# Eight of seventeen one-hot matrices per body made by ScalarE instead of VectorE, in a two-layer graph network with attention and experts

## The reference, cut to what matters

```python
def _rgcn_layer(X, W, root, bias, gamma, beta, src, dst, etype, inv_deg):   # first stage, four layers
    h = jnp.einsum('ni,rio->rno', X, W)
    msg = h[etype, src] * inv_deg[:, None]
    agg = jax.ops.segment_sum(msg, dst, num_segments=X.shape[0])
    out = agg + X @ root + bias
    ...                                       # layer norm, gamma, beta
    out = jax.nn.elu(out)
    return out + X

all_h = jnp.einsum('ni,rio->nro', h, weight)  # second stage, once, eight relations, no weights
msg = all_h[src, rel]
agg = jax.ops.segment_sum(msg, dst, num_segments=h.shape[0])
```

## Time and profile before

| | |
|---|---|
| Three runs | 8418.92, 8429.41 (median), 8451.86 us |
| The profiled execution | 8445.94 us, of which the span from first to last instruction is 8444.1 us |
| Granted TensorE clock, mean | 0.832 of full |
| Busy, share of the span | TensorE 5985.2 us, 71%; VectorE 4887.0 us, 58%; GpSimd 4238.0 us, 50%; ScalarE 1584.5 us, 19% |
| Four layers | from 622.7 to about 5522 us |
| Last graph stage | about 6530 to 7576 us |
| One-hots L524 and L526 | 3332 and 833, 1127.5 and 225.2 us busy |
| Sums L544 | 4165, 1746.5 us busy |
| Gathers L515 | 4165, 4015.2 us busy |
| Step products L559 | 3142.9 us busy |

### The profile page before, as it was taken

The page is one execution under the profiler, slowest core; times in us unless marked ns, Lnnn a source line. Parts: engine busy times, 40 slices in busy tenths (PEclk is TensorE's granted clock), DMA queues, the critical chain, the costliest instruction groups (busy, mean ns, idle before and its releaser), DMA issues. The chain is left out here.

```text
span 8444.1 us, 107673 instructions
## 1 busy us (share of the span) xinstructions
PE 5985.2 (71%) x18474; PEld 3592.9 (43%) x18474; DVE 4887.0 (58%) x16836; ACT 1584.5 (19%) x3834; POOL 4238.0 (50%) x4288
## 2 busy tenths in 40 slices
PE   0587777767777767777776777778488677664398
PEld 0244444444544444444443333345334444443265
DVE  7106666667777767777776677732433666662412
ACT  0231112211111113333330000022021111110132
POOL 0007677756666656666656777710000777762211
PEclk9799899988788888889887666679699888877699
DMA  1324444433333333434434333300034333330000
GB/s 54 127 93 124 120 125 124 125 118 113 112 112 114 113 117 114 118 116 119 119 111 127 104 104 104 103 24 0 0 129 138 105 105 105 105 92 2 12 14 17
DMA packets 457906, 797.23 MB, mean 94 GB/s; under 512 B 87260, under 2 KB 322100, under 8 KB 457609
## 3 DMA queue, kind: packets, MB, share of 16 engines
q0 software_dynamic: 200480, 548.02, 22.9%
q1 hardware_dynamic: 257382, 248.75, 8.9%
HBM read 606.70 MB, written 189.74 MB: 94 GB/s over the span
## 5 line engine op out<-in xcount | busy, mean ns | idle before, releaser
L515 POOL DMA_INDIRECT gnn_msg<-tables,gnn_row_ring x4165 | 4015.2, 964 | 2346.5 <-issue 1644.2
L559 PE MATMUL bank<-gnn_msg,gnn_hot 128*128 128x256 f32 x8330 | 3142.9, 496 | 1292.5 <-DVE sums L544 1030.5
L559 PEld LDWEIGHTS bank<-gnn_msg,gnn_hot 128*128 128x128 f32 x8330 | 1715.7, 235 | 2586.6 <-DVE sums L544 1928.3
L544 DVE TENSOR_TENSOR sums<-sums,bank 128x256 f32 x4165 | 1746.5, 419 | 1587.6 <-PE bank L559 1127.2
L524 DVE TENSOR_SCALAR gnn_hot<-iota,gnn_meta_ring 128x128 f32<-128x128 f32 x3332 | 1127.5, 356 | 332.0 <-ACT gnn_meta_ring L508 332.0
L133 POOL TENSOR_TENSOR ve<-mv,eps 128x7 f32<-128x7 f32 x35 | 7.2, 205 | 1348.3 <-DVE mv L127 1199.7
L652 PE MATMUL bank<-gnn_w,residual 128*128 128x512 f32 x1176 | 572.5, 611 | 1.4 <-ACT residual L668 1.4
L507 ACT COPY gnn_row_ring<-row 128x9 int32 (+1 forms) x490 | 97.8, 200 | 1512.7 <-PE bank L559 1498.8
L1698 PE MATMUL bank<-tables_w,sums 128*128 128x512 f32 x784 | 338.3, 593 | 6.4 <-ACTq L117 6.4
L652 PEld LDWEIGHTS bank<-gnn_w,residual 128*128 128x128 f32 x1176 | 237.2, 202 | 174.7 <-issue 152.9
L672 ACT COPY residual<-bank 128x512 f32<-128x512 f32 x294 | 172.3, 586 | 681.3 <-PE bank L652 681.3
(11 more groups left out here) (398 smaller groups left out, 6804.7 us busy)
## 6 DMA issues: line engine op xcount, KB each, us to landing
tables<-residual SPq DMA_DIRECT2D x294, 256.0 KB, 2.7
gnn_msg<-tables,gnn_row_ring POOLq DMA_INDIRECT x4165, 2.8
tables<-sums SPq DMA_DIRECT2D x98, 512.0 KB, 2.9
tables<-gnn_msg SPq DMA_DIRECT2D x98, 256.0 KB, 2.1
residual<-first_norm SPq DMA_DIRECT2D x98, 128.0 KB, 3.1
first_norm<-state SPq DMA_DIRECT2D x1, 6272.0 KB, 20.8
first_rows<-residual SPq DMA_DIRECT2D x1, 6272.0 KB, 39.0
mixer_rows<-residual SPq DMA_DIRECT2D x49, 128.0 KB, 2.4
```

What stands on the lines that cost most here:

```text
L515: self.nc.gpsimd.indirect_dma_start(out=self.msg[:, s0 + u, :], out_offset=None, in_=table, in_offset=bass.IndirectOffsetOnAxis(ap=self.ro ...
L544: self.nc.vector.tensor_tensor(at, at, self.sums(s), ALU.add).then_inc(self.added, 1)
L559: self.nc.tensor.matmul(self.sums(s), self.hot[:, s, :], self.msg[:, s, :], start=True, stop=True).then_inc(self.summed, 1)
```

## The change

`ACT_HOTS` (4) of the one-hots of each half are made by ScalarE, in `ring`, behind its two copies. The distance |column - node| goes to a new buffer `away` (Abs with the scale -1 and the node's number as bias); the one-hot is Relu(weight - weight x distance), for which a third column of `meta_ring` holds the negated weights. Without weights it is Relu(1 - distance). VectorE makes the first five one-hots of the first half and the first four of the second, nine in a body where it made seventeen, by a new `NEXT_HOTS`; `begin_vector` makes five. TensorE waits for one of two counters, according to who made the one-hot. The rest of the program is the same.

```diff
-NEXT_HOTS = (((), (0,), (1,), (2,), (3,), (4,), (5,), (6,), (7,)),
-             ((), (), (0, 1), (2,), (3,), (4, 5), (6,), (7, 8)))
+DVE_HOTS = (5, 4)
+ACT_HOTS = 4
+NEXT_HOTS = (((), (), (0,), (), (1,), (), (2,), (), (3,)),
+             ((), (), (0,), (1,), (), (2,), (3,), (4,)))
...
     def ring(self, act, i, n, h):
 
         s0, w = HALVES[h]
+        m = self.meta_ring[:, h, 0:w, :]
         act.wait_ge(self.summed, n * SLOTS + (s0 + w))
         gate(act, self.c)
         at = ds(i * SLOTS + s0, w)
         self.nc.scalar.copy(self.row_ring[:, h, 0:w], self.rows[:, at]).then_inc(self.ring_ready, 1)
-        self.nc.scalar.copy(self.meta_ring[:, h, 0:w, :], self.c.meta[:, at, :]).then_inc(self.ring_ready, 1)
+        self.nc.scalar.copy(m[:, :, 0:2], self.c.meta[:, at, :]).then_inc(self.ring_ready, 1)
+        act.wait_ge(self.ring_ready, n * 4 + (2 * h + 2))
+        gate(act, self.c)
+        for k in range(ACT_HOTS):
+            u = DVE_HOTS[h] + k
+            self.nc.scalar.activation(self.away[:, k, :], self.c.iota[:], ACT.Abs, bias=m[:, u, 0:1], scale=-1.0)\
+                .then_inc(self.away_ready, 1)
+        if self.weighted:
+            self.nc.scalar.mul(m[:, :, 2], m[:, :, 1], -1.0).then_inc(self.away_ready, 1)
+        else:
+            act.sem_inc(self.away_ready, 1)
+        act.wait_ge(self.away_ready, (n * 2 + (h + 1)) * (ACT_HOTS + 1))
+        gate(act, self.c)
+        for k in range(ACT_HOTS):
+            u = DVE_HOTS[h] + k
+            to = self.hot[:, s0 + u, :]
+            if self.weighted:
+                ins = self.nc.scalar.activation(to, self.away[:, k, :], ACT.Relu, bias=m[:, u, 1:2], scale=m[:, u, 2:3])
+            else:
+                ins = self.nc.scalar.activation(to, self.away[:, k, :], ACT.Relu, bias=self.c.ones[:, 0:1], scale=-1.0)
+            ins.then_inc(self.act_hot_ready, 1)
...
     def begin_vector(self, dve, n):
 
         dve.wait_ge(self.ring_ready, n * 4 + 2)
-        for u in range(HALF):
+        for u in range(DVE_HOTS[0]):
             self.one_hot(0, u)
...
     def tensor(self, pe, n, after):
         for s in range(SLOTS):
             pe.wait_ge(self.landed[s], n * 16 + 16)
-            pe.wait_ge(self.hot_ready, n * SLOTS + s + 1)
+            h = 0 if s < HALF else 1
+            u = s - HALVES[h][0]
+            if u < DVE_HOTS[h]:
+                pe.wait_ge(self.hot_ready, n * sum(DVE_HOTS) + (h * DVE_HOTS[0] + u + 1))
+            else:
+                pe.wait_ge(self.act_hot_ready, n * 2 * ACT_HOTS + (h * ACT_HOTS + u - DVE_HOTS[h] + 1))
```

More of the change, by code:

```diff
@@ L489, in __init__, with use @@
         self.landed = [c.sem(f"message{s}_landed") for s in range(SLOTS)]
[L490 to L495, removed]
+        self.ring_ready, self.hot_ready, self.summed, self.added, self.away_ready, self.act_hot_ready = (
+            c.sem(n) for n in ("slots_copied", "hot_made", "steps_summed", "steps_added", "distances_made", "scalar_hot_made"))
+    def use(self, msg, hot, away, row_ring, meta_ring, rows, weighted):
+        self.msg, self.hot, self.away = msg, hot, away
         self.row_ring, self.meta_ring, self.rows, self.weighted = row_ring, meta_ring, rows, weighted
@@ L1076, in gnn0 @@
         row_ring = sb("row_ring", [P, 2, HALF], I32)
-        meta_ring = sb("meta_ring", [P, 2, HALF, 2], F32)
+        meta_ring = sb("meta_ring", [P, 2, HALF, 3], F32)
+        away = sb("away", [P, ACT_HOTS, P], F32)
         own = sb("own", [P, 2 * D + 11], F32)
@@ L1086, in gnn0 @@
         edges = c.edges = EdgeSum(nc, c)
-        edges.use(msg, hot, row_ring, meta_ring, c.row4, True)
+        edges.use(msg, hot, away, row_ring, meta_ring, c.row4, True)
         post = Post(nc, c, ph, cutter(own), scratch, vecs, w, brow)
@@ L1883, in gnn1 @@
     with Phase(nc, "gnn1") as ph:
-        msg, hot, row_ring, meta_ring = (ph.sb(n, s, d) for n, s, d in (
+        msg, hot, row_ring, meta_ring, away = (ph.sb(n, s, d) for n, s, d in (
             ("msg", [P, SLOTS, D], F32), ("hot", [P, SLOTS, P], F32), ("row_ring", [P, 2, HALF], I32),
-            ("meta_ring", [P, 2, HALF, 2], F32)))
+            ("meta_ring", [P, 2, HALF, 3], F32), ("away", [P, ACT_HOTS, P], F32)))
         edges = c.edges
-        edges.use(msg, hot, row_ring, meta_ring, c.row4, False)
+        edges.use(msg, hot, away, row_ring, meta_ring, c.row4, False)
         keys = Keys1(nc, c, ph, wt)
```

## The result

The changed kernel takes 8296.77 us (median; 8293.46 to 8304.74), the kernel before 8439.37 us beside it. The ratio is 0.9835, 95% interval 0.9811 to 0.9858: 1.65% faster, 142.6 us, where 106 us (8323 us) had been forecast. The profiled execution took 8293.46 us, 152.5 us less than the profiled one of before. In the changed file the step's matmul is L587 (was L559), the gather L538 (L515), and L617 is L645, L652 is L680, L658 is L686, L668 is L696, L845 is L873 and L1033 is L1061.

What follows compares the result with a forecast made beforehand. VectorE's order of work was taken to bound layers one to three, gathers the rest; gains of 24 + 47 + 35 = 106 us off 8429.4 gave 8323 us, 1.3% faster, range 8255 to 8430 us (forecast's own 8289 to 8382).

Steps and rivals of the forecast that it cites:

- places count and not busy time: VectorE's sequence: a one-hot in a 0.63 us gap between sums is free; one with work behind costs 0.22 to 0.25 us.
- Layer two, 0.97 x 48 = 47 us: Layer two: one-hots leaving steps 1, 7, 11 and 14 win 0.97 us per body, all on the path, 47 us.
- steps 11 and 14 win nothing: Layer one, second half of a body: sums wait for TensorE, so only the first half's 0.50 us counts, 24 us.
- half of 0.44: Layer three: 0.50 us in the first half, half of 0.44 us in the second, where TensorE may be awaited; 35 us.
- I cost this part at nothing: ScalarE's added work, about 3.1 us per half body, is hidden behind other waits and costs 0 in the likeliest case.
- The push on L845: Layer three after the second ring: ScalarE's work delays L1033 and TensorE's L845 by 1.5 us, hidden with 0.6 us to spare.
- (c): Rival, slower: ScalarE becomes the link, losing (x - 3.9) x 144 at x us per half; 8525 us at 5.3; chance 0.10.
- Fourth layer and last graph stage at the floor: Both stages are paced by GpSimd's gathers, seventeen in about 21.3 us per body, so they gain 0.
- (a): Rival, hidden: VectorE's freed time is waited out for TensorE in layers one to three; 12 us gain, 8417 us; chance 0.18.
- (b): Rival, all of it: each one-hot costs 0.25 us, 2.0 us per body; 282 us gain, 8147 us; chance 0.10.

Runs made afterwards that it cites:

- the free and the exposed places: Kernel before without four one-hots in gaps (behind steps 3, 5, 13, one of 16): 8444.7 us; without four charged ones (1, 7, one each of 11, 14): 8318.8 us.
- VectorE's part alone: Changed kernel's VectorE table with nine one-hots, ScalarE making none and the other eight matrices left zero: 8311.5 us, ratio 0.9852 to the kernel before.
- the four exposed one-hots gone: Kernel before without the one-hots behind steps 1 and 7 and one of two behind 11 and 14: 8318.8 us, ratio 0.9855.
- with it alone added: Kernel before, VectorE still making all seventeen one-hots, ScalarE also making its eight into a buffer nobody reads: 8431.6 us, ratio 0.9997.
- the six added matmuls: Kernel before plus six matmuls nobody reads per body of layer three, behind step 13 on TensorE: 8391.0 us, ratio 0.9946.
- 6.1 us per half: Changed kernel with ScalarE's four Abs of each half done three times, on the slower chip: 10065.9 us, ratio 1.0266 to the kernel before.

## Why the prediction was right, and where it was off

- **VectorE's order is the limit, places count and not busy time.** Shown by the free and the exposed places. In the means over a layer's bodies, the interval from a sum to the next fell behind step 1 by 0.27 to 0.32 us and behind 7 by 0.26 in layers one to three; in two and three it fell behind 11 by 0.26 and 0.22, behind 14 by 0.22, behind 16 by 0.03, and behind 3, 5 and 13 not at all, each within 0.07 us of its term. Two terms of the sum were mis-sized all the same, both for the second half of a body.
- **Layer two, 0.97 x 48 = 47 us.** Measured 49.
- **Layer one, "steps 11 and 14 win nothing", 0.50 x 48 = 24 us.** Measured 35 us, 0.73 per body, which this layer's spread of 10 us hardly tells from 24. With VectorE's part alone it gave 48 us, and with the four exposed one-hots gone 47, 1.0 per body, so the second half wins too and this term was too small. There the interval behind step 14 fell by 0.22 us and the one behind 15 grew by as much, as a wait for TensorE would have it; but behind 11 the 0.22 us stayed won, and 12 and 13 fell by 0.3 us together. The earlier trace rows show one wait of 1.47 us for TensorE in one body, and I took that body for all 48. Why 12 and 13 fell was not tested; the mean granted clock of the layer rose from 0.92 to 0.96. ScalarE's part took 13 us back, near the spread; I had costed it at nothing by a place of layer three.
- **Layer three, "half of 0.44", 0.72 x 48 = 35 us.** Measured 56. VectorE's part alone gave 31, near the 35, but not by the halving: steps 11 and 14 gave their 0.44 us in full, and the interval behind step 15 grew by 0.48 and took it all back. That the sum came out was luck. The other 26 us came with ScalarE's work: with it alone added, the matmuls behind step 15 go from 530 to 442 ns and the layer loses 27 us. The step that failed is "I cost this part at nothing", in the layer if not over the kernel: the prediction has no term for TensorE's clock. The counts of fast and slow bodies show that the clock carries the gain, and the six added matmuls that it is worth time by itself; how ScalarE's delay makes more bodies fast stays open.
- **The push on L845.** Forecast 1.5 us more wait for ScalarE in layer three; its wait at this place is 2.67 us, in before 0.95. It stayed hidden but for 0.12 us behind step 9, which neither part alone shows; 6 us in the layer. The cover isn't endless: at 6.1 us per half layer three has run out of it. (c) put its end at 3.9 us, or 3.7 with the 0.25 us that the prediction takes off elsewhere; where it lies between 3.3 and 6.1 us was not measured. Layers one and two hardly lose, and (c) had taken one price for all three.
- **Fourth layer and last graph stage at the floor.** -4 and -2 us, as forecast.
- **The rivals.** (a) and (b) are refuted; (c) is a real mechanism that this change, at 3.3 us per half, doesn't reach in sum on the chips that ran it. The Trainium skill (ScalarE: Activation LUTs, Rules for kernel authors) keeps relu and the like on VectorE. The price per operation bears it out (390 and 482 ns for 340), the changed kernel's time does not: two operations on an engine with room beat one on the engine whose order is the limit.

## What to carry to other kernels

Before moving work off a busy engine, list where each piece stands: here one that fitted into a gap between dependent operations was free, and one with work behind it cost 0.22 to 0.32 us. Moving the rest into gaps gave 89 us here with no operation changed. A cost of zero over the whole kernel can be two of opposite sign in two stages, so read each stage, don't take one body for all of a stage, and look how much an unchanged stage varies before reading a small difference.

## What the runs showed of the hardware

Six added matmuls per body made 49 bodies shorter by 45 us in all: with them the granted clock over layer three (3130 to 4380 us) is 0.95, 0.87 without, and 128x256 matmuls behind them take 379 ns in place of 530. ScalarE's new work did a like thing without added matmuls: the fast bodies of layer three went from 12 to 34. The other is the slower chip: the same program, the same 0.17 us operations, but in the last stage's chain 0.7 and 1.4 us from one start to the next in place of 0.2, and 16% more time. A gain that rests on VectorE's exact order was seen on two chips at 8437 to 8439 us; on this one the one version with ScalarE's one-hots and no added Abs, which also had the added matmuls in layer one, lost 0.6%.
